# An adapter kernel with sorted tiles: the prologue's loads move to one queue, its low halves to VectorE

## The reference, cut to what matters

```python
# x: (64, 64, 512) f32, 64 batches of 64 rows; itok: (64,) int32, the expert of each batch, 1 or 2 here
# E = 3 experts; W_down (3, 512, 256), W_up (3, 256, 512), biases and layer-norm weights per expert
e = itok
h = einsum('bsh,bhk->bsk', x, W_down[e]) + b_down[e][:, None, :]
h = gelu(h, approximate=False)
h = einsum('bsk,bkh->bsh', h, W_up[e]) + b_up[e][:, None, :]
h = x + h
h = (h - mean(h)) * rsqrt(var(h) + 1e-5)        # over the last axis
out = h * ln_w[e][:, None, :] + ln_b[e][:, None, :]
```

## Time and profile before

| | |
|---|---|
| median of 3 runs | 151.52 us (150.98 to 151.83) |
| profiled execution | span 150.9 us, from its first to its last instruction |
| TensorE busy | 127.5 us, 84% of the span |
| VectorE busy | 124.2 us, 82% |
| ScalarE busy | 89.5 us, 59% |
| POOL busy | 108.7 us, 72% |
| moved by DMA | 23.10 MB, mean 153 GB/s |
| mean granted TensorE clock | 0.962 of full speed |

### The profile page before, as it was taken

One profiled execution on the slowest core, in us unless ns is written; L12 is line 12 of the kernel. 1 busy time (PEld: TensorE's weight loads), 2 busy tenths in 40 slices (PEclk: granted clock), 3 DMA queues, 4 the chain that ended last, 5 costly groups with the idle time before them and its releaser, 6 DMA issues.

```text
span 150.9 us, 4104 instructions
## 1 busy us (share of the span) xinstructions
PE 127.5 (84%) x822; PEld 111.2 (74%) x823; DVE 124.2 (82%) x299; ACT 89.5 (59%) x205; POOL 108.7 (72%) x112
## 2 busy tenths in 40 slices
PE   0038564999999999999999999999999999999640
PEld 0037564999989998988988888888888888897310
DVE  0486343656699999998999999899999999999895
ACT  3261234257777676666666676777676767665531
POOL 3263080198888888988988888888888888889641
PEclk9999786599999999999999999999999999999998
DMA  4930899999755445444445555545554222221455
GB/s 127 309 125 15 250 277 300 270 246 262 206 173 172 141 139 143 139 141 141 139 139 149 155 154 151 154 147 153 156 160 119 70 70 70 74 72 35 104 139 141
DMA packets 13469, 23.10 MB, mean 153 GB/s; under 512 B 2320, under 2 KB 3856, under 8 KB 13456
## 3 DMA queue, kind: packets, MB, share of 16 engines
q1 hardware_dynamic: 9840, 17.72, 41.2%
q10 hardware_dynamic: 3616, 5.25, 12.6%
HBM read 14.57 MB, written 8.65 MB: 154 GB/s over the span
## 4 chain that ended last, share of the span: by engine, by line
DVE 48%; issue 17%; DVEq 12%; PE 10%; DMA 7%; SPq 3%; POOL 1%; ACT 0%; ACTq 0%
DVE res L597 19%; DVE r L560 13%; DVEq L184 8%; DVE hb L547 5%; PE h_ps L689 5%; DMA bd_rows<-in_L_cond_b_down_dram 4%; PE y_ps L715 3%; DMA itok_all_i<-in_itok_B_dram 3%; DVE gT_lo L553 3%; DVE xT_lo L540 2%; PE xT_ps L677 1%; SPq L255 1%; DVE even_count L504 1%; DVE var_eps L573 1%; DVEq L597 1%
## 5 line engine op out<-in xcount | busy, mean ns | idle before, releaser
L343 POOL TENSOR_TENSOR scaled<-centred,lnw_rows 128x512 f32<-128x512 f32 x31 | 40.8, 1316 | 14.9 <-ACT centred L415 8.2
L328 POOL TENSOR_TENSOR xb<-x_sb,bu_rows 128x512 f32<-128x512 f32 x33 | 42.6, 1297 | 7.1 <-DMA bu_rows<-in_L_cond_b_up_dram 7.1
L597 DVE SCALAR_TENSOR_TENSOR res<-scaled,rstd,lnb_rows 128x512 f32<-128x512 f32 x33 | 44.2, 1339 | 1.0 <-POOL rstd L334 0.5
L407 ACT ACTIVATE sq_junk<-r,r_nmean 128x512 f32<-128x512 f32 x33 | 23.9, 724 | 34.4 <-DVE r_nmean L567 34.4
L390 ACT CAST xT_hi<-xT_ps 128x512 fp32r<-128x512 f32 x33 | 18.7, 567 | 11.6 <-PE xT_ps L677 11.6
L540 DVE TENSOR_TENSOR xT_lo<-xT_ps,xT_hi 128x512 fp32r<-128x512 f32 x33 | 22.5, 682 | 3.3 <-ACT xT_hi L390 3.3
L689 PE MATMUL h_ps<-wd_hi,xT_hi 128*128 x132 | 24.9, 312 | 0.0
L715 PE MATMUL y_ps<-wu_hi,gT_hi 128*128 x66 | 23.9, 444 | 0.7 <-ACT gT_hi L400 0.7
L560 DVE SCALAR_TENSOR_TENSOR r<-y_ps,xb 128x512 f32<-128x512 f32 x33 | 22.4, 679 | 2.4 <-PE y_ps L715 1.4
L415 ACT ACTIVATE centred<-r,r_nmean 128x512 f32<-128x512 f32 x31 | 22.4, 723 | 1.4 <-DVE r_nmean L567 1.4
L677 PE MATMUL xT_ps<-ident,x_sb 128*128 128x128 f32 x132 | 20.7, 281 | 2.5 <-DMA x_sb<-in_x_dram 2.5
(11 more groups left out here) (65 smaller groups left out, 141.6 us busy)
## 6 DMA issues: line engine op xcount, KB each, us to landing
x_sb<-in_x_dram SPq DMA_DIRECT2D x66, 128.0 KB, 3.0
out_dram<-res ACTq DMA_DIRECT2D x33, 128.0 KB, 2.3
out_dram<-res SPq DMA_DIRECT2D x33, 128.0 KB, 2.6
wu<-in_L_cond_W_up_dram SPq DMA_DIRECT2D x3, 512.0 KB, 7.1
wd<-in_L_cond_W_down_dram ACTq DMA_DIRECT2D x2, 512.0 KB, 5.7
bu_rows<-in_L_cond_b_up_dram SPq DMA_DIRECT2D x1, 768.0 KB, 8.8
lnw_rows<-in_L_cond_ln_w_dram SPq DMA_DIRECT2D x1, 768.0 KB, 9.5
lnb_rows<-in_L_cond_ln_b_dram SPq DMA_DIRECT2D x1, 768.0 KB, 10.7
```

What stands on the lines that cost most here:

```text
L328: pool.tensor_tensor(xb[:, c % DEEP, :], x_sb[:, c % FAR, :], bu_rows[:, ds(e * H, H)], ALU.add).then_inc(xb_ready, 1)
L343: pool.tensor_tensor(scaled[:, c % DEEP, :], centred[:, c % PAR, :], lnw_rows[:, ds(e * H, H)], ALU.mult).then_inc(scaled_ready, 1)
L407: act.activation(sq_junk[:], r[:, c % DEEP, :], ACT.Square, bias=r_nmean[:, c % DEEP:c % DEEP + 1], accum_out=sq_sum[:, c % DEEP:c % DEEP ...
L597: dve.scalar_tensor_tensor(out=res[:, c % FAR, :], in0=scaled[:, c % DEEP, :], scalar=rstd[:, c % DEEP:c % DEEP + 1], in1=lnb_rows[:, ds(e ...
```

## The change

itok's load becomes the first DMA of ACT's queue; all six weight loads follow it there, wd(0), wd(1), wd(2), wu(0), wu(1), wu(2). SP begins with its wait, now for `slots_ready` 1, and issues `bd_rows` directly behind x(0). POOL makes no low halves; VectorE makes all three `wd_lo` behind the sort and `wu_lo` of expert 1 between `x_lo(1)` and `wu_low(2)`. There are 8 warm-ups instead of 11 behind the sort's matmul.

```diff
-    WARM_UPS_BEFORE, WARM_UPS_AFTER = 11, 3
+    WARM_UPS_BEFORE, WARM_UPS_AFTER = 8, 3
@@ block.sync
-            sp.dma_start(itok_all_i[:], rows_of(itok, B)).then_inc(itok_in, 16)
-            load_w_down(sp, 1)
-            load_w_up(sp, 0)
-            sp.wait_ge(slots_ready, 2)
+            sp.wait_ge(slots_ready, 1)
...
             load(0, 0, entries(0, 0, 2))
-            load_w_up(sp, 1)
+            sp.dma_start(bd_rows[:], rows_of(b_down, P)).then_inc(bd_in, 16)
             load(1, 1, entries(1, 0, 2))
-            sp.dma_start(bd_rows[:], rows_of(b_down, P)).then_inc(bd_in, 16)
-            load_w_up(sp, 2)
             load(2, 2, entries(2, 0, 2))
@@ block.gpsimd
-            for e in range(E - 1):
-                pool.wait_ge(w_hi_ready, e + 1)
-                w_down_low(pool, e).then_inc(wd_lo_ready, 1)
-
-            pool.wait_ge(w_hi_ready, E + 2)
-            w_up_low(pool, 1).then_inc(wu_lo_ready, 1)
             pool.wait_ge(slots_ready, 2)
@@ block.scalar
-            load_w_down(act, 0)
-            load_w_down(act, 2)
+            act.dma_start(itok_all_i[:], rows_of(itok, B)).then_inc(itok_in, 16)
+            for e in range(E):
+                load_w_down(act, e)
+            for e in range(E):
+                load_w_up(act, e)
@@ block.vector
-            dve.wait_ge(w_hi_ready, E)
-            w_down_low(dve, E - 1).then_inc(wd_lo_ready, 1)
+            for e in range(E):
+                dve.wait_ge(w_hi_ready, e + 1)
+                w_down_low(dve, e).then_inc(wd_lo_ready, 1)
...
             x_lo(1, 1)
+            wu_low(1)
             wu_low(2)
```

## The result

The changed kernel takes 147.5 us (147.37 to 148.84), the kernel before on the same chip 151.65; the ratio is 0.9745 with a 95% interval of 0.9691 to 0.9799, and 0.9768 (0.9724 to 0.9811) in a second set of runs. That is 3.5 to 3.9 us less, where 5.8 were forecast: faster as said, inside the range, but 1.8 us short of the likeliest time.

A forecast was written before the change was run, and what follows sets the result against it. Steady state, 3.59 us a tile, stays; its start, set by the prologue, moves. Tile 0's chain gives 5.9, bu_rows 5.7, lnb_rows 6.4 to 7.1; smallest, with 0.1 for reserve, 5.8: 151.5 − 5.8 = 145.7 us, range 143.8 to 148.6.

The forecast's parts named there:

- The sort: Prologue: SP released at 6.6 us, 6.0 earlier, with 2.4 from itok, 1.9 from even_count and 1.7 from tile_expert.
- credit for itok: Part of the sort's gain: itok heading ACT's queue takes 2.4 us instead of 4.9, releasing SP 2.4 us earlier.
- x(0): First tile's load beside the weights: 4.2 us, landing at 12.4; gT_ps(0) then 4.9 to 5.3 us earlier.
- rival (a): SP's queue: x(0), bd and x(1) starve behind the weights; gain 2.5 to 4 us, 148.2 us; chance 0.15.
- The clock: TensorE from gT_ps(0) to the end of y(0): full clock gives up to 2 us, 1 us counted.
- The DMA stream: Without the DMA pause, bu_rows allows a start 5.2 to 6.2 us earlier, lnb_rows 6.4 to 7.1.
- The sum: Smallest middle of the three gates decides: 5.8 us off the 151.5 us run time, 145.7 us; chance 0.58.
- (d): Steady state: VectorE against POOL settles in another phase, slower; at 0.3 us a tile, 155.3 us; chance 0.04.
- (b): Prologue: everything lines up, 2.4 GHz from gT_ps(0) on, only the DMA pause counts; gain 7.1 to 8, 144.0 us; chance 0.11.
- (c): Sort gains nothing from itok's place, release at 9.1; gain 3.5 to 4.5 us, 147.5 us; chance 0.12.

The follow-up runs named there:

- e3: The kernel before with all low halves on VectorE and none on POOL; ratio 0.9794.
- e4: The kernel before with SP waiting for slots_ready 1 instead of 2; ratio 0.9887.
- f5: The changed kernel with itok's load back on SP's queue, the only load there ahead of SP's wait; ratio 0.9751.
- f1: The changed kernel with wu(1) and wu(2) back on SP's queue, behind x(0) and bd_rows and behind x(1); ratio 0.9731.
- f2: The changed kernel with 20 warm-up matmuls behind the sort instead of 8; ratio 0.9656.
- g1: The changed kernel with x(1) issued ahead of bd_rows on SP's queue; ratio 0.9716.
- g2: The changed kernel with x(1) ahead of bd_rows, the low half of wu(1) back on POOL and 24 warm-ups; 146.43 us, ratio 0.961.
- a0: The changed kernel once more, unaltered, as base of the comparisons; ratio 0.9768.
- f6: The changed kernel with the low half of wu(1) back on POOL; ratio 0.9752.
- g4: The changed kernel with SP waiting for slots_ready 2 instead of 1; ratio 0.9685.
- e2: The kernel before with itok's load moved from SP's queue to the head of ACT's; ratio 0.9793.

## Why the prediction was right in kind and 1.8 us off

**The sort.** Right in each term: itok in 2.44 us (2.4 forecast), the two stalled steps at 0.17 and 0.10 (0.2), SP released at 6.69 (6.6), wd_lo from 9.14 to 12.64 (9.2 to 12.9). That the stalls were POOL's is shown by e3, which takes POOL's subtractions away, and by e4, where another step is hit. Its credit for itok was wrong in worth, not in size: f5 takes the 2.1 us of release back at no cost.

**x(0).** Mis-sized: 12.4 forecast, 14.6 measured, 6.27 us behind its second issue where I took 4.2. x(0) landed behind wu(1) (13.3) and ahead of the end of wu(2) (17.4); f1, with 1 MB less of them in front, had it at 11.4. That is the mechanism of rival (a), and its times for x(0) (14.5 to 15.8), for gT_ps(0) (21.3) and its gain (2.5 to 4) are those measured; its x(1) at 19 or later and its "no faster clock" are not. The Trainium skill's rule that an engine drains a whole packet before it changes queues ("DMA: Bandwidth & Descriptors", section "Queues, rings and completion order") points the same way, but as I had applied it, one packet for each half, it gave 12.4 too; no run here shows single packets' turns. Then came x(1) (18.3, forecast 17.6) and gT_ps(0) at 21.21 (19.4 to 19.8).

**The clock.** I counted on 1 us of a possible 2 behind gT_ps(0). The slow stretch moved ahead of it, and from 20 us on the clock was full: from the start of gT_ps(0) to the first residual it was 31.1 − 24.65 = 6.5 us before and is 25.16 − 21.21 = 3.95 now, 2.5 us less. Some 0.2 of that is bu_rows being early: y(0) was ready at 30.9 before and at 25.1 now. This term made good what x(0) had lost. No run here changed the clock alone, so the split between clock and other causes isn't shown.

**The DMA stream.** bu_rows landed at 22.0 (forecast 23.2 to 24.1) and lnb_rows at 32.7 (33.6 to 34.6): in the two profiles of the changed kernel both were early enough not to count, so their part as its limit was wrong there. It was a near thing: in f1, f2, g1 and g2, where bu_rows landed at 21.3 to 24.8, r(0) waited 0.7 to 1.1 us for it.

**The sum.** The prediction names 25.8 for the first residual, but its own sum, 31.14 less 5.8, is 25.3; in the same way its first `res` is 35.2 and not 34.8, and lnb_rows, at 33.6, allows 7.4 and not 7.1. The first residual came at 25.2 and 26.0 in two profiles, and the span was 145.5 and 146.6: the shift of the first profile, 6.0 us, was nearly as forecast. The step that missed is the one about the profiled execution's own time, "the runs of the kernel lie between 150.98 and 151.83 with a median of 151.52, so at most 0.9 above it". It takes 151.5 − 150.9 = 0.6 us as what a run adds to its span; the runs show 1.7 to 1.8 for this kernel and 2.0 for the changed one. By that the profiled execution took about 152.7 us, 1.1 above its median: I took the shift from a long execution and the base from the median. The 1.8 us are then 1.4 for this term, 0.6 for the stretch behind the first residual (120.3 for 119.8), less 0.2 for a first residual earlier than the sum had it. Why the stretch behind is longer stays open. And that the first residual came so near its forecast has luck in it, as x(0) and the clock were off in opposite directions.

**The rivals.** (d) is out: the pace stayed at 3.60. (b) is out by its time, though its full clock from gT_ps(0) on did come. (c) named 147.5 us, the time measured, but its reason is out: itok took 2.44 us, and SP was released at 6.7 and not 9.1. Open is why the last of the 16 DMA engines is late by so differing amounts: bu_rows, issued at the same point, was in at 21.3 to 24.1 in the profiles of the changed kernel and its near relatives (a0, f2, f6, g1, g2, g4), while the middle one of its 16 pieces came at 19.2 to 20.7. No experiment here separated that.

## What to carry to other kernels

Before a shift read from one profile is taken off a median, check that the profiled execution was a typical one; here some 1.1 us of a 5.4 us difference in spans was, by the runs' times, its own length. In this kernel the small load that starts everything was fast when neither queue had a large one issued with it, not because it headed its queue, and the first tile's load, issued beside megabytes of weights, came so late that an issue 2.1 us earlier bought nothing (f5). Short VectorE steps on a critical chain should not run beside POOL's elementwise work on SBUF, and moving that work or a transfer shifts the collision to another step, so look for what the freed engine starts next.

## What the runs showed of the hardware that I had not expected

- A 16 KB load of 64 rows took 2.4 to 2.9 us with both queues empty at its issue, 4.5 to 5.5 us with a 512 KB load issued on the other queue within 0.01 us of it, whichever of the two queues it was on (the kernel before, e2 to e4, f5).
- A VectorE step of 0.1 to 0.3 us took 1.8 to 2.3 us when it started behind a POOL subtraction of 2.34 us, and which step it was hung on 0.6 us in wd(0)'s landing: `even_count` in the kernel before, `same_before` in e4, which differs from it only behind that point. `io_table`, started in the same time as `tile_expert`, was not held (0.21).
- With the clock granted in full, down(0) took 1.68 us beside 2.56 at half. In f2 a pause of TensorE of 3.15 us ahead of x(0) was followed by a fall to 1.2 GHz; in the changed kernel, with 5.03 us, it had fallen by 13 us; in g2, with 24 warm-ups and a pause of 1.01 us, it stayed full.
- A row's granted clock can be wrong: g4's says 1.00 for the stretch below, in which down(0) took 2.56 us, as in the changed kernel at 0.50. The durations of the matmuls are the check.

```profile
14.50:19.50 5.00, 4.31 (x21) 4.34 (x22) 1.82 (x2) 1.53 (x2) 0.00 (x0) 1.00 1.04 255
```
